# Dividing the probabilities by their row sums on VectorE instead of GpSimd, in the cross attention of layer 1

## What is computed

```
def _gqa(q, k, v):
    scores = einsum('bsghd,btgd->bghst', q, k) / sqrt(d)
    p = softmax(scores, axis=-1)
    return einsum('bghst,btgd->bsghd', p, v)

q, qx, k, v  = fp8-rounded inputs @ weights        # q, qx: 16 heads; k, v: 8 groups; d = 128
kx, vx       = split(cond @ w_kv_x)                # 8 groups each
q, qx, k, kx = layer norm of each head
cat  = concat(_gqa(q, k, v), _gqa(qx, kx, vx))     # 32 heads of 128
catq = round_to_fp8(cat / proj_smooth)
out  = (catq @ wproj.T) * scale                    # added to x
```

## Time and profile before

| | before |
|---|---|
| median of 3 runs | 3867.37 us (3865.74 to 3867.59) |
| the profiled execution's own time | 3872.02 us |
| its span, first to last instruction | 3870.2 us |
| busy: TensorE, VectorE, ScalarE, GpSimd | 3219.4, 2455.9, 1590.5, 350.6 us |
| the products on GpSimd (line 3344) | 128, 133.2 us |
| granted TensorE clock, mean over the span | 0.905 |

### The profile page before, as it was taken

How to read it: one execution, slowest core, us unless ns; L and a number is a source line. 1 busy time by engine, 2 the same in 40 slices (tenths; PEclk the granted TensorE clock), 3 DMA queues, 4 the chain that set the end, 5 groups by cost and what they waited for, 6 DMA issues and landing times. The chain is left out here.

```text
span 3870.2 us, 77187 instructions
## 1 busy us (share of the span) xinstructions
PE 3219.4 (83%) x28495; PEld 2294.9 (59%) x28496; DVE 2455.9 (63%) x6356; ACT 1590.5 (41%) x3970; POOL 350.6 (9%) x353
## 2 busy tenths in 40 slices
PE   7899999544586999899998994788996889767799
PEld 6566666311364666665666662567886767654488
DVE  6655555588686666666666657767883178567433
ACT  2243444377343555555555552223342244321111
POOL 2000000000051111111111110001000000000000
PEclk9899999755697999999999996897788999898999
DMA  2000000000400000000000003000000000006100
GB/s 96 30 20 19 23 16 14 1 0 0 137 22 2 3 1 1 3 1 3 1 1 3 1 2 94 1 1 19 14 11 0 0 1 0 22 22 163 47 9 11
DMA packets 89572, 79.05 MB, mean 20 GB/s; under 512 B 16640, under 2 KB 82752, under 8 KB 88896
## 3 DMA queue, kind: packets, MB, share of 16 engines
q1 hardware_dynamic: 88208, 75.57, 6.5%
q10 hardware_dynamic: 1200, 1.11, 0.1%
HBM read 74.57 MB, written 2.10 MB: 20 GB/s over the span
## 5 line engine op out<-in xcount | busy, mean ns | idle before, releaser
L3118 PE MATMUL bank<-L1w_w,L1x_xqT 128*128 128x512 f32 x640 | 304.5, 599 | 2.1 <-DVE L1x_xqT L3386 2.1
L3392 DVE TENSOR_REDUCE L1x_ssq<-L1x_square 128x4 f32<-128x512 f32 x192 | 131.6, 685 | 185.9 <-ACT L1x_square L3245 180.0
L1046 DVE TENSOR_REDUCE L0x_top<-bank 128x4 f32<-128x512 f32 x256 | 159.3, 684 | 103.9 <-PE bank L972 100.8
L1031 ACT ACTIVATE L0x_P<-bank,L0x_level 128x512 f32<-128x512 f32 x256 | 155.2, 689 | 158.0 <-PE bank L992 158.0
L3269 ACT ACTIVATE L1x_square<-bank,L1x_top 128x128 f32<-128x128 f32 x512 | 182.2, 375 | 19.5 <-DVE L1x_top L3414 19.5
L3179 PE MATMUL bank<-L1w_wp,L1x_catb 128*128 128x256 bf16 x1536 | 188.4, 273 | 0.1
L3344 POOL TENSOR_TENSOR L1x_square<-L1x_square,L1x_total 128x512 f32<-128x512 f32 x128 | 133.2, 1041 | 604.6 <-DVE L1x_total L3420 604.6
L3245 ACT ACTIVATE L1x_square<-bank 128x512 f32<-128x512 f32 x192 | 115.0, 599 | 146.4 <-PE bank L3118 146.4
L3118 PEld LDWEIGHTS bank<-L1w_w,L1x_xqT 128*128 128x128 f32 x640 | 115.4, 192 | 99.5 <-issue 95.0
L3179 PEld LDWEIGHTS bank<-L1w_wp,L1x_catb 128*128 128x128 bf16 x1536 | 150.2, 98 | 35.2 <-issue 17.1
L888 DVE TENSOR_TENSOR x_sb<-x_sb,bank 128x256 f32 (+1 forms) x112 | 47.0, 420 | 194.1 <-PE bank L208 183.8
(11 more groups left out here) (647 smaller groups left out, 7793.1 us busy)
## 6 DMA issues: line engine op xcount, KB each, us to landing
L0x_mask<-in_maskrows SPq DMA_DIRECT2D x16, 512.0 KB, 3.2
L3w_wgu<-in_L_ffn_Wg SPq DMA_DIRECT2D x8, 704.0 KB, 8.5
L3w_wgu<-in_L_ffn_Wu SPq DMA_DIRECT2D x8, 704.0 KB, 9.7
L1a_wp_quarter<-in_L_xattn_wproj SPq DMA_DIRECT2D x4, 1024.0 KB, 5.8
L3x_ctxT<-in_ctxT SPq DMA_DIRECT2D x32, 128.0 KB, 2.1
L3w_wd<-in_L_ffn_Wd SPq DMA_DIRECT2D x8, 512.0 KB, 8.6
L0x_ctxT<-in_ctxT SPq DMA_DIRECT2D x16, 128.0 KB, 2.9
L1w_w<-in_L_xattn_wq SPq DMA_DIRECT2D x1, 2048.0 KB, 9.6
```

The lines of the kernel that those rows point to most:

```text
L1031: act.activation(self.P[:, i % 2, r, :], self.work_bank[r][:, :], ACT.Exp, bias=self.level[:, :]).then_inc(self.p_ready.sem, 1)
L1046: dve.tensor_reduce(self.top[:, s, 16 * c + 4 * r:16 * c + 4 * r + 4], self.work_bank[r][:, :].rearrange("p (h k) -> p h k", h=4), X, ALU.max,
L3118: last = pe.matmul(made_bank[n % 4][:, :], inputs(SOURCE[n], k), w[:, k, 4 * n:4 * n + 4, :], start=(k == 0), stop=(k == C - 1))
L3392: dve.tensor_reduce(ssq[:, 4 * n:4 * n + 4], square[:, (n + 2) % 3, :].rearrange("p (h e) -> p h e", h=4), X, ALU.add).then_inc(sum_ready. ...
```

## The change

VectorE multiplies the tile by the reciprocals itself, right behind its reciprocal; GpSimd's `share` and the semaphore between the two are gone. `step` makes VectorE wait for its reciprocal before the product, which reads it.

```diff
-            def share(b, m):
-                pool.wait_ge(inv_ready.sem, inv_ready.after(b, m + 1))
-                rows = P[:, m % 3, :].rearrange("p (h k) -> p h k", h=4)
-                pool.tensor_tensor(rows, rows, total[:, 4 * m:4 * m + 4].unsqueeze(2).to_broadcast([128, 4, 128]),
-                                   ALU.mult).then_inc(shared.sem, 1)
-
             step.restart()
             shift_x(0)
             with pool.Fori(0, B - 1) as b:
                 step.restart()
                 shift_x(b + 1)
-                for m in range(MG):
-                    share(b, m)
-            for m in range(MG):
-                share(B - 1, m)
...
                 def invert(m):
                     dve.wait_ge(p_ready.sem, p_ready.after(b, m + 1))
                     part = total[:, 4 * m:4 * m + 4]
-                    dve.reciprocal(part, part).then_inc(inv_ready.sem, 1)
+                    step(dve.reciprocal(part, part))
+                    rows = P[:, m % 3, :].rearrange("p (h k) -> p h k", h=4)
+                    dve.tensor_tensor(rows, rows, part.unsqueeze(2).to_broadcast([128, 4, 128]), ALU.mult).then_inc(shared.sem, 1)
```

More of the change, by code:

```diff
@@ L3089, in L1_xattn @@
         v_made, v_ready = ph.batch_sem("v_made", 4), ph.batch_sem("v_ready", 4)
-        scored, top_found, p_ready, inv_ready, shared, p_turned, pT_ready, mixed, o_read, cat_ready, left = (
-            ph.batch_sem(n, MG) for n in ("scored", "top_found", "p_ready", "inv_ready", "shared", "p_turned", "pT_ready", "mixed", "o_read",
+        scored, top_found, p_ready, shared, p_turned, pT_ready, mixed, o_read, cat_ready, left = (
+            ph.batch_sem(n, MG) for n in ("scored", "top_found", "p_ready", "shared", "p_turned", "pT_ready", "mixed", "o_read",
                                           "cat_ready", "left"))
```

## The result

The changed kernel takes 3900.23 us (median of 6 runs, 3894.59 to 3905.0), the kernel before 3866.73 beside it (6 runs, 3857.17 to 3871.47). The ratio is 1.0085, with an interval from 1.0074 to 1.0096. The change costs 33 us. The forecast had the side right and the size at less than half: 14.6 us, and 3900 lies above the range.

What follows compares the result with a forecast made beforehand. VectorE and TensorE were taken as bound in a ring in steps 1 to 5, TensorE leading from step 6; 0.91 us in each of 16 batches, 14.6 us, on the median 3867.37 gave 3882.0 us, range 3871 to 3891.

Steps and rivals of the forecast that it cites:

- The ring: Loop of reciprocal, product, turn, mix, read-out, rounding: VectorE becomes the bound of steps 2 to 5, at 4.10 us each.
- TensorE from step 6 on: From step 6 to the batch's end TensorE sets the pace again, 0.91 us late, with nothing added.
- The head: Step 0 of a batch: the turn starts 0.39 us earlier, worth nothing because ScalarE's copy behind it starts no sooner.
- the first part: The paragraph on what bounds the kernel now, which took the granted clock as full from one batch's windows.
- 0.91 us in each of 16 batches: The sum over the whole kernel: the delay of step 5's turn, counted in every batch, 14.6 us.
- The ring term: Cost of VectorE's longer steps 2 to 5: 0.91 us a batch, 14.6 us in all, the forecast's whole sum.
- A: Rival: product cheaper than its nearest row, or VectorE's lateness absorbed in waits; -2 to +5 us, chance 0.13.
- B: Rival: VectorE's wait on its own result or the product costs more; +24 us, 3891 us, chance 0.09.
- C: Rival: faster, since the shorter way from reciprocal to turn decides; -19 us, 3848 us, chance 0.08.

Runs made afterwards that it cites:

- e11: The changed kernel with 6 transposes of the identity added before the first mix of each batch: 3890.05 us, ratio 1.0074.
- e4: The changed kernel with reciprocal and product of step m + 2 moved ahead of the rounding of step m: 3858.63 us, ratio 0.9972.
- e8: The kernel before with 5 transposes of the identity added in each batch before the projection `make(3)`: 3882.07 us, ratio 1.0031.
- e6: The kernel before with 9 transposes of the identity added in each batch before the projection `make(3)`: 3885.95 us, ratio 1.0049.

## Why the prediction was wrong in size

- **The ring was right.** Step 4.10 forecast, 4.13 measured; product 0.684 and 0.692; own wait 0.04 in both. The reciprocal of step 5 comes 20.30 us into the batch instead of 18.92, 1.38 late (forecast 1.30), its turn 1.00 late (0.91). A batch is 0.99 longer (0.91), since the step is 0.03 longer three times.
- **TensorE from step 6 on was right in its end.** The forecast had the product of step 6 "in time for the matmul". The weights of that turn wait 0.41 for it, but TensorE is busy all the time from there (16.44 of 16.44). VectorE catches up at the read-out of step 7 (it waits 1.57), not at that of step 6.
- **The head was not "worth nothing".** The 0.39 is gained and lost as forecast, but the head is where the clock falls. The earlier turn has moved 0.39 of idle time from ahead of the turn to ahead of the first mix (0.50 to 0.88), and e11 shows that the falls of 10.2 us come with that gap.
- **The step that failed** is in the first part: "All at full granted clock (1.00, the 2.4 GHz level)". It was read from the windows of one batch and carried to 16. The kernel before already had the clock at 0.50 in 6 heads, as its batch 2 shows at 0.93, and "0.91 us in each of 16 batches" has no term for it. That term is 16.0 us in the traces (18 in the medians, 33.5 less 15.4, which scatter more). The ring term beside it was right to about 1 us: 14.78 over 15 batches is 15.8 over 16, against 14.6. A forecast of the clock's term from the kernel before alone would have been a range and no number: the count went from 6 to 8, 11 and 14 with batch lengths less than 1 us apart.
- **The rivals.** A and B didn't come: the product has the price of its nearest row, and the own wait costs 0.04. The 33 us lie on B's side, beyond its 24, but for another cause. C did not come, for the reason given against it. In e4 the same product on VectorE is faster than both kernels as soon as it stands ahead of the rounding, so the order decides; whether C's shorter way has a part in that, these runs don't separate.

## What to carry to other kernels

Look at the granted clock in the windows of every pass of a loop before one pass is multiplied by their number, and where TensorE idles in one place of each pass, put a price on the fall that may come there; eight dummy transposes held the clock here, in all batches but one, and cost an undisturbed batch nothing. When work moves to an engine in a ring, what stands ahead of it in the queue counts more than the engine's total. Ask also what the other engine's work runs beside: the same product was free beside PSUM reads and cost 0.76 us beside a 16-bit operation in SBUF.

## What the runs showed of the hardware

A wait of 2.1 to 2.7 us on TensorE was followed by a granted clock of 0.50 in some passes of a loop and not in others, for 3.4 us, or for 10.2 with a further gap of 0.6 to 0.8 us behind it. Making a batch longer by 0.55 us (e8) took the falls from 6 to 8 in the profiled execution, and by 0.98 (e6) to 11. A 16-bit `tensor_scalar` on VectorE went from 0.29 to 1.05 us beside GpSimd's product, while f32 reads from PSUM stayed at 0.66 to 0.69.
